# Every large tile at a multiple of 512 bytes, and new orders for the fill, the turn and the drain

## The chip, the cores and the metric

The kernel runs on one core of a Trainium2 chip. Its time is the device time of one execution in microseconds; each figure is the median of several runs. The profile is one further execution, taken by the hardware profiler.

## The reference

128 samples, each with 128 nodes of 256 features (`x`) and a weighted 128 x 128 matrix (`adj`). Four graph layers follow one another, each on the normalised and rectified features and with a residual:

```python
h = jnp.maximum(_layernorm(x, axis=-1), 0.0)
x = x + L0(h, adj, ...)   # hypergraph convolution, relu, layer norm, hypergraph convolution, + h
h = jnp.maximum(_layernorm(x, axis=-1), 0.0)
x = x + L1(h, adj, ...)   # tanh(norm(adj) @ h @ W + b)
h = jnp.maximum(_layernorm(x, axis=-1), 0.0)
x = x + L2(h, adj, ...)   # attention: exp(leaky(8 tanh((s_i + s_j) / 8))) * adj, rows rescaled, @ h @ w
h = jnp.maximum(_layernorm(x, axis=-1), 0.0)
x = x + L3(h, adj, ...)   # three layers adj @ (h @ W) + b, relu after the first two
```

All arrays are float32.

## The kernel before

Two samples (J = 2) lie side by side in a pass, and four streams A, B, C and D each take one pass after another; 16 groups of four passes make 64 passes, called units below. Each unit goes through 16 steps on TensorE (PE). A step named U multiplies by the graph's matrix in float32 (eight instructions of 128 columns; 1U has sixteen), a step named W by a weight matrix. For W each operand is split into a high and a low part of type fp32r (UHI and ULO, WHI and WLO), and the product is the sum of three: twelve matmuls of 256 columns, in 0W twelve of 512, in 1W twenty-four of 256. G makes the hypergraph's matrix, 3S spreads the attention scores, 5U works on rows with the split of T (THI, TLO). Behind every U, ScalarE (ACT) copies the result to UHI and VectorE (DVE) writes what is left to ULO; the second half of the next W waits for it. Behind every W comes a residual sum, statistics on DVE (0S, 1S, ...), a norm on GpSimd (POOL; N0 to N3, NZ) and the normalising copy on ACT (H0, 1W, 2X, 3W).

The order of each engine's work is written out by hand in the table `ORDER` (line 20): for PE, ACT, DVE, POOL and the load queue (SP) a first list, a turn that is repeated, and a last list. `ordered` (line 63) gives the n-th occurrence of a step to stream n modulo 4. The engines run in order and meet at semaphores alone, so a step that waits holds up all behind it on its engine. A turn holds one unit's steps, each of another stream or pass, so that a chain of one stream spans several turns. With the counts in the lists there are 55 turns on PE.

Names of the steps: B and G on ACT build and copy the hypergraph's matrices; `high` and `low` split a weight matrix on ACT and DVE; `shifts` (PE, once) and `centred` (DVE, once) fold the layer norm's parameters into W2 and hold one of the two wide banks until done; SH, R and TH on ACT are the residual's shift, the row sums of adj, and the high part of T; DA to DD on DVE turn degrees into factors; 2N, RX, RB, RH on POOL are weighting and residual sums. PE begins with 18 warm-up matmuls of ones.

SBUF tiles are laid out one after another in the order in which `sb(...)` is called (lines 99 to 177), each start rounded up to 32 bytes. In the kernel before, small tiles such as `COLS` (40 bytes), `L3B1C` (8) and the four constants (8 each) stand among the large ones, and `BHT` and `G` have 1040 bytes, so what follows them starts at odd places:

```python
WLO = {step: sb(f"WLO{step}", [P, *shape], F32R) for step, shape in WIDTH.items()}
COLS = sb("COLS", [P, 2 * HC + DC])
GAMMA, BETA, ACOL = COLS[:, 0:HC], COLS[:, HC:2 * HC], COLS[:, 2 * HC:]
B1 = sb("B1", [P, DH])
```

Of the kernel before, what the change touches and what calls it, by code (L numbers as in the profile page):

```python
# [6 lines left out]
F32 = mybir.dt.float32  # L7
F32R = mybir.dt.float32r
ACT = mybir.ActivationFunctionType
P = 128  # L10
J = 2
STREAMS = ("A", "B", "C", "D")
# [14 lines left out]
    "ACT": (  # L27
# [8 lines left out]
    "DVE": (  # L36
# [22 lines left out]
}  # L59


# [13 lines left out]
def program(nc, xs, adj_t, adj_r, w1t, w2t, l1w, l2w, l2wt, l3w1, l3w2, l3w3, cols, b1, b2, l1b, l3b1, l3b2, l3b3, out):  # L75
# [6 lines left out]
    with ExitStack() as ctx:  # L82
# [30 lines left out]
        def per_stream(name, *shape, dt=F32):  # L113
            return {s: sb(f"{name}_{s}", [P, *shape], dt) for s in STREAMS}
# [762 lines left out]
```

## Time and profile before

| | |
|---|---|
| median of 3 runs | 1374.74 us (1374.6 to 1374.94) |
| the profiled execution, its span | 1375.02 us, 1373.2 us |
| mean granted clock of TensorE | 0.997 |
| PE busy | 1348.1 us, 98% |
| PE's weight loads (PEld) | 1293.4 us, 94% |
| DVE, ACT, POOL busy | 1202.0 (88%), 1112.6 (81%), 1037.1 us (76%) |
| chain that ended last | PE 83%, DVE 10%, issue 3%, ACT 3%, POOL 1% |

The profiled execution's own time is 1.8 us above its span, which goes from the first to the last instruction. Matmuls overlap one another, so the distance between starts tells more than the busy time of one. The timeline merges equal instructions that follow each other; the bracket behind a row is the idle time of the engine before it and what ended it.

### The profile page before, as it was taken

What the parts mean: (1) busy time and instruction counts of PE and PEld (TensorE: products, weight loads), DVE (VectorE), ACT (ScalarE), POOL (GpSimd) and SP (SyncE); (2) the same over time, 40 slices, a digit from 0 to 9 for tenths busy, and PEclk for the clock granted to TensorE, in tenths of its full rate; (3) what the DMA queues carried; (4) which work ended last, traced back from release to release, by engine and by line L of the source; (5) the groups of instructions that cost most, each with busy time, mean ns of one, the idle gap of its engine ahead of it and who ended that gap; (6) DMA issues with size and microseconds to landing.
All of it is one profiled execution on the core that took longest, in us unless ns stands there. A gap on an engine that the chain in (4) does not pass through costs nothing.

```text
span 1373.2 us, 32422 instructions
## 1 busy us (share of the span) xinstructions
PE 1348.1 (98%) x10552; PEld 1293.4 (94%) x10552; DVE 1202.0 (88%) x3607; ACT 1112.6 (81%) x2824; POOL 1037.1 (76%) x2067
## 2 busy tenths in 40 slices
PE   8989999999999999999999999999999999999988
PEld 7879999999999999999999999999999999999987
DVE  6887988988988988988988989889889889889876
ACT  5787888888888888888887888888887888888875
POOL 5867778777777777777777777777787787777762
PEclk9999999999999999999999999999999999999999
DMA  6011111112111111111111111111111111121100
GB/s 200 13 29 54 32 36 56 47 36 55 48 36 55 48 36 56 47 36 53 49 36 48 55 36 48 43 48 47 44 48 47 37 54 48 36 55 47 36 9 32
DMA packets 83351, 64.37 MB, mean 47 GB/s; under 512 B 40560, under 2 KB 65648, under 8 KB 83184
## 3 DMA queue, kind: packets, MB, share of 16 engines
q1 hardware_dynamic: 83184, 62.29, 15.7%
q8 instruction: 86, 1.41, 0.4%
q14 instruction: 81, 0.66, 0.2%
HBM read 45.49 MB, written 16.78 MB: 45 GB/s over the span
## 4 chain that ended last, share of the span: by engine, by line
PE 83%; DVE 10%; issue 3%; ACT 3%; POOL 1%; DVEq 0%; POOLq 0%; ACTq 0%
PE BANK L394 20%; PE BANK L326 18%; PE BANK L401 12%; PE WIDE L394 8%; PE WIDE L337 8%; PE BANK L353 4%; PE WIDE L401 4%; PE BANK L358 2%; PE BANK L311 2%; PE BANK L370 1%; PE BANK L373 1%; PE BANK L369 1%; PE BANK L412 1%; DVE BN_B L594 1%; DVE ST_A L615 1%
## 5 line engine op out<-in xcount | busy, mean ns | idle before, releaser
L635 DVE TENSOR_TENSOR ULO_C<-BANK,UHI_C 128x512 fp32r<-128x512 f32 x112 | 76.5, 683 | 25.0 <-ACT UHI_C L539 15.8
L635 DVE TENSOR_TENSOR ULO_D<-BANK,UHI_D 128x512 fp32r<-128x512 f32 x112 | 76.4, 682 | 24.1 <-ACT UHI_D L539 13.0
L635 DVE TENSOR_TENSOR ULO_A<-BANK,UHI_A 128x512 fp32r<-128x512 f32 x112 | 76.5, 683 | 23.2 <-ACT UHI_A L539 11.8
L635 DVE TENSOR_TENSOR ULO_B<-BANK,UHI_B 128x512 fp32r<-128x512 f32 x112 | 76.5, 683 | 21.0 <-ACT UHI_B L539 12.3
L478 ACT ACTIVATE UHI_D<-BANK 128x512 fp32r<-128x512 f32 x96 | 57.1, 595 | 40.5 <-PE BANK L326 37.3
L478 ACT ACTIVATE UHI_A<-BANK 128x512 fp32r<-128x512 f32 x96 | 57.2, 596 | 39.6 <-PE BANK L326 38.5
L478 ACT ACTIVATE UHI_C<-BANK 128x512 fp32r<-128x512 f32 x96 | 57.1, 595 | 38.7 <-PE BANK L326 34.8
L478 ACT ACTIVATE UHI_B<-BANK 128x512 fp32r<-128x512 f32 x96 | 57.1, 595 | 35.9 <-PE BANK L326 34.5
L761 POOL TENSOR_TENSOR LN_A<-LN_A,MHALF 128x2 f32<-128x2 f32 x80 | 56.5, 706 | 1.3
L757 POOL TENSOR_TENSOR LN_B<-MV_B,EPS 128x2 f32<-128x2 f32 x80 | 15.6, 195 | 55.0 <-DVE MV_B L602 54.9
L447 ACT ACTIVATE H_A<-RES_A,LN_A 128x256 f32<-128x256 f32 x96 | 52.4, 597 | 5.4 <-POOL LN_A L769 5.0
L534 ACT ACTIVATE BANK<-BANK,L3B1C 128x256 f32<-128x256 f32 x128 | 51.9, 443 | 5.9 <-PE BANK L358 3.1
L761 POOL TENSOR_TENSOR LN_C<-LN_C,MHALF 128x2 f32<-128x2 f32 x80 | 55.5, 694 | 1.3
L761 POOL TENSOR_TENSOR LN_B<-LN_B,MHALF 128x2 f32<-128x2 f32 x80 | 55.5, 694 | 1.2
L761 POOL TENSOR_TENSOR LN_D<-LN_D,MHALF 128x2 f32<-128x2 f32 x80 | 55.5, 694 | 1.3
L447 ACT ACTIVATE H_C<-RES_C,LN_C 128x256 f32<-128x256 f32 x96 | 52.4, 598 | 1.7 <-POOL LN_C L769 1.6
L447 ACT ACTIVATE H_B<-RES_B,LN_B 128x256 f32<-128x256 f32 x96 | 52.3, 597 | 1.3 <-POOL LN_B L769 1.3
L757 POOL TENSOR_TENSOR LN_A<-MV_A,EPS 128x2 f32<-128x2 f32 x80 | 15.6, 195 | 49.9 <-DVE MV_A L602 49.9
L447 ACT ACTIVATE H_D<-RES_D,LN_D 128x256 f32<-128x256 f32 x96 | 52.3, 596 | 0.8 <-POOL LN_D L769 0.3
L757 POOL TENSOR_TENSOR LN_C<-MV_C,EPS 128x2 f32<-128x2 f32 x80 | 15.6, 195 | 48.8 <-DVE MV_C L602 48.8
L757 POOL TENSOR_TENSOR LN_D<-MV_D,EPS 128x2 f32<-128x2 f32 x80 | 15.6, 195 | 47.7 <-DVE MV_D L602 47.7
L594 DVE BATCH_NORM_STATS2 BN_A<-RES_A 128x6 f32<-128x256 f32 x96 | 35.6, 411 | 1.5 <-POOL RES_A L811 1.5
(519 smaller groups left out, 6053.6 us busy)
## 6 DMA issues: line engine op xcount, KB each, us to landing
X_A<-in_xs SPq DMA_DIRECT2D x16, 256.0 KB, 2.8
X_B<-in_xs SPq DMA_DIRECT2D x16, 256.0 KB, 2.9
X_C<-in_xs SPq DMA_DIRECT2D x16, 256.0 KB, 3.0
X_D<-in_xs SPq DMA_DIRECT2D x16, 256.0 KB, 3.0
out_rows<-O_A SPq DMA_DIRECT2D x16, 256.0 KB, 2.0
out_rows<-O_B SPq DMA_DIRECT2D x16, 256.0 KB, 2.1
out_rows<-O_C SPq DMA_DIRECT2D x16, 256.0 KB, 2.0
out_rows<-O_D SPq DMA_DIRECT2D x16, 256.0 KB, 2.0
```

What stands on the lines that cost most here:

```text
L326: last = nc.tensor.matmul(bank(s, step, k)[:, at:at + P], lhs[s][:, j, m * P:(m + 1) * P], rhs(s, j), start=True, stop=True)
L337: last = nc.tensor.matmul(bank(s, "1U", k)[:, j, m * P:(m + 1) * P], Z[s][:, j, m * P:(m + 1) * P], GZ[s][:, j, :], start=True, stop=True)
L353: nc.tensor.matmul(dst, w[:, m, q * P:(q + 1) * P], UHI[s][:, m * n:(m + 1) * n], start=(w is lo and m == 0), stop=False)
L394: nc.tensor.matmul(dst, UHI[s][:, at[m]:at[m] + P], w[:, m, :], start=(w is lo and m == 0), stop=False)
L401: last = nc.tensor.matmul(dst, ULO[s][:, at[m]:at[m] + P], hi[:, m, :], start=False, stop=(m == chunks - 1))
L447: nc.scalar.activation(dst[s][:, j, :], src[s][:, j, :], ACT.Relu, bias=LN[s][:, NB, j:j + 1], scale=LN[s][:, RSTD, j:j + 1]).then_inc(sem ...
L478: nc.scalar.activation(UHI[s][:, 0:J * D], bank(s, step, k)[:, :], ACT.Copy).then_inc(sem(f"c{step}"), 1)
L534: last = nc.scalar.activation(half, half, ACT.Relu, bias=L3B1C[:, q:q + 1])
L594: last = nc.vector.bn_stats(BN[s][:, j, :], src[s][:, j, :])
L635: nc.vector.tensor_tensor(ULO[s][:, 0:J * D], bank(s, step, k)[:, :], UHI[s][:, 0:J * D].bitcast(F32), ALU.subtract).then_inc(sem(f"l{step ...
L757: nc.gpsimd.tensor_tensor(ve, MV[s][:, :, 1], EPS[:, :], ALU.add).then_inc(sem("ve" + tag), 1)
L761: nc.gpsimd.tensor_tensor(rstd, ve, MHALF[:, :], ALU.pow)\
```

## The change

The tiles of a multiple of 512 bytes are asked for first, behind the 384 bytes of `ST`, which bring the first of them to a multiple of 512; the odd-sized ones (BHT, DIAG, G, COLS, the constants, the statistics) come last. No tile changes its size, and no instruction its operands. The first and last lists of all five engines are new. The turn lists of PE, ACT, DVE, POOL and SP stand in the diff as they were. The lists of ACT, DVE and SP are cut to the first one here, POOL's are left out.

```diff
@@ -19,43 +19,42 @@
 
 ORDER = {
     "PE": (
-         "G 0U G 0W shifts 0U G 0W 0U 1U 1W 1U G 0W 1W 0U 2U 0W 2W 1U 1W 2U 1U 2W 1W 3S 2U 3U 2W 3W 2U 3S 2W 3U 4U 3W 3S "
-         "4W G 5W 3U 4U 5U G 3W 6U 4W 6W 0U 5W 3S 0W 5U 4U 6U 4W 3U 6W 1U 0U 1W 5W 3W 0W 2U G 5U 2W 6U 1U 1W 4U 6W",
+         "G 0U G 0W 0U shifts G 0W 1U 0U 1W 0W G 1U 2U 1W 2W 0U 1U 0W 2U 1W 3S 2W 1U 3U 1W 3W 2U 3S 2W 4U 3U 4W 2U 3W G 5W "
+         "2W 3S 5U 4U 4W 6U 3U 6W 5W 3W 0U 3S 5U 0W 4U G 3U 6U 4W 6W 1U 1W 0U 5W 3W 0W 2U 5U G 2W 6U 1U 1W 4U 6W",
          "0U 4W 3S 0W 2U 5W 3U 2W 5U 3W G 6U 1U 1W 4U 6W",
-         "0U 4W 3S 0W G 3U 5W 2U 3W 5U 2W 1U 6U 4U 1W 4W 6W 0U G 5W 0W 5U 2U 3S 6U 2W 6W 1U 0U 3U 0W 1W 3W 3S 1U 2U 1W 2W "
-         "4U 3U 4W 3W 2U 2W 5W 4U 3S 4W 3U 5U 3S 3W 3U 5W 3W 5U 4U 6U 4W 4U 6U 5W 4W 6W 5U 5W 6W 5U 6U 6U 6W 6W"),
+         "G 0U 3S 4W 0W 3U 2U 5W 2W 5U 3W 1U 6U 1W G 4U 6W 0U 3S 4W 0W 5W 2U 3U 5U 2W 6U 1U 6W 0U 3W 0W 1W 3S 1U 1W 2U 3U "
+         "4U 2W 3W 2U 4W 2W 5W 4U 3S 4W 5U 3U 5W 3S 3W 3U 6U 3W 6W 4U 5U 4U 4W 4W 6U 5W 5W 5U 6W 5U 6U 6U 6W 6W"),
     "ACT": (
-         "B G high H0 B 0U G 0W H0 B 0U G high H0 0Z SH 0W 1U B 0Z SH high 0U 1U SH H0 G 0W high R 1W 0U 2U TH SH R 0Z 0W "
-         "high 1U 2W 0Z 1W high 2U 2X 1U R 2Y high 2W TH 3T 3E 1W 2U 3U 2X 1W 2W 2Y 2U 3T 3E 3W 2X 3U 2W 4U 2Y B 3T 3E 4W "
-         "4V G 3W R 5W B 3U 2X 4U 5U G H0 TH 6U 4W 4V 2Y TH 0U H0 3T 5W SH 3W 3E 5U 4U 0W 6U 4W 0Z 4V 3U 1U R SH B 0U 5W "
-         "H0 1W 0W 2U 5U 0Z 2W TH 6U",
+         "B H0 high G B 0U G H0 0U 0W B H0 G R 0Z high SH TH 1U 0U high 0W B high SH 0Z 0W 1W 1U SH high 2U high G H0 TH "
+         "0Z 2W 0U SH 1U 1W 2X 2U 0W 2Y 3T 3E 0Z 2W 1U 3U R high TH 2X 1W 2Y 2U 3T 3E 3W 2W 4U B 1W 3U 4W 4V 2X 2U R G 2Y "
+         "5W 3T 3W 3E 4U 2W 5U H0 4W 6U 4V TH 3U R 2X 5W 2Y 0U 3T 3E B 3W 5U 4U 0W G 6U 3U SH 0Z 4W 1U 4V H0 R 0U 5W B SH "
+         "1W 0W 2U H0 5U 0Z 2W TH 6U",
...
     "DVE": (
-         "T X XA DA DB DC T low spread 0U X DA scaled 0W DD DB XA X T XA 0S centred DC 0U 0A T low 0W DD 0S 0A 1U DA DB X "
-         "XA 1W DC 0U DD 1U 1S 0W 1A 0S DA 0A DB 1W DC 1S 0U DD 1A low 2U 0W 0S 2W 0A 1U low 2S 2A 1W 2U 1S 1A low 1U 2W "
-         "1W 1S 2S 2A 3L 3E 3R 1A 3I 2U 3J 3U 2W T 3W 3S 3A 2S 2A 2U 3L 3E 3R 2W 3I low 3U 3J T 4U 2S 3W 3S 3A 3L low 4V "
-         "3R 3E 2A X 3I DA 5W XA 3U 5U 3J 4U X DB DC DA 3W 6U 3S 3A DB XA 4V 6W DC 0U T DD 5W 0W 5U 3L 3E 3R 4U 0S 3I 0A "
-         "6U 4V 3U X 1U DD XA 6W 1W 0U 1S 1A 5W 3J 3W 3S 0W 0S 2U 0A 5U 2W T 3A 2S 2A 1U DA 6U 1W DB DC 1S DD 4U 6W 0U 1A "
-         "X",
+         "T X XA spread T DA low X DB XA DC 0U scaled 0W T X DA XA 0S 0A DB DD 0U T DC DD centred X DA 0W low XA 1U 0U 0S "
+         "DB 1W 0A 1S DC 1A 0W 0S low DD 0A 1U low 2U 1W 1S 2W DA 1A DB DC DD 0U 2S 2A low 1U 0W 2U 0S 0A 1W 1S 2W 3L 3R "
+         "3E 2S 1A 3I 2A 1U 3U 3J low 1W T 3W 3S 3A 2U 1S 3L 1A 2W 3E 3R 4U 2S 3I 2A 3U T 3J 4V 3W 2U 3S 3A low 5W X DA XA "
+         "2W 5U 4U 3L 3R DB 2S 3I 3E 2A 6U 4V DC 3J 3U X 6W DD 5W 3W 3S 3A 0U 5U 3L 3R T 3E 0W 4U 0S 0A 6U DA 3I 3U XA DB "
+         "6W X 1U 4V 1W 1S DC 3J 1A DD 0U 5W XA 3W 0W 0S 2U 0A 5U 2W T 3S 3A 2S 2A 1U DA 6U 1W DB 4U 6W DC DD 1S 1A 0U X",
...
     "SP": (
-         "W F F D X W F F R W X F X D D R X T T O X O R D O D W X T F T W",
+         "F X F W D R W W F F X R X D T R D X O T O X X T O F D W D T W F",
...
@@ -96,22 +95,20 @@
         WIDTH = {"0W": (DC, DH), "1W": (HC, D), "2W": (DC, D), "3W": (DC, D), "4W": (DC, D), "5W": (DC, D), "6W": (DC, D)}
         W_STEPS = tuple(WIDTH)
         U_STEPS = tuple(f"{i}U" for i in range(7))
+        def per_stream(name, *shape, dt=F32):
+            return {s: sb(f"{name}_{s}", [P, *shape], dt) for s in STREAMS}
+
+        ST = per_stream("ST", 12, J)
+        CNT, CNM, BE, DNM, DNI, DN, S2, DG1, DINV, S8, RSR, RSA = range(12)
         WHI = {step: sb(f"WHI{step}", [P, *shape], F32R) for step, shape in WIDTH.items()}
         WLO = {step: sb(f"WLO{step}", [P, *shape], F32R) for step, shape in WIDTH.items()}
-        COLS = sb("COLS", [P, 2 * HC + DC])
-        GAMMA, BETA, ACOL = COLS[:, 0:HC], COLS[:, HC:2 * HC], COLS[:, 2 * HC:]
         B1 = sb("B1", [P, DH])
         B2, L1B, L3B2, L3B3 = (sb(n, [P, D]) for n in ("B2", "L1B", "L3B2", "L3B3"))
-        L3B1C = sb("L3B1C", [P, DC])
         BW = sb("BW", [P, D])
         WA = sb("WA", [P, D])
         SPREAD = sb("SPREAD", [P, HC + DC, P])
         IDENT = sb("IDENT", [P, P])
         ONES = sb("ONES", [P, P])
-        MONE, MHALF, LEAST, EPS = (sb(n, [P, J]) for n in ("MONE", "MHALF", "LEAST", "EPS"))
-
-        def per_stream(name, *shape, dt=F32):
-            return {s: sb(f"{name}_{s}", [P, *shape], dt) for s in STREAMS}
 
         X = per_stream("X", J, D)
 
@@ -123,11 +120,8 @@
         THI = per_stream("THI", J, P, dt=F32R)
         TLO = per_stream("TLO", J, P, dt=F32R)
 
-        BHT = per_stream("BHT", J, P + 2)
-        DIAG = per_stream("DIAG", J)
         HT = per_stream("HT", J, P)
         AT = per_stream("AT", J, P)
-        G = per_stream("G", J, P + 2)
         GZ = per_stream("GZ", J, P)
         H = per_stream("H", J, D)
         H0 = per_stream("H0", J, D)
@@ -138,14 +132,21 @@
         TMP = per_stream("TMP", J, D)
         AE = per_stream("AE", J, P)
         O = per_stream("O", J, D)
+        JUNK = per_stream("JUNK", J, P)
+        W1, W2, W2G = sb("W1", [P, DC, DH]), sb("W2", [P, HC, D]), sb("W2G", [P, HC, D])
+        RAW6W = sb("RAW6W", [P, DC, D])
+        BHT = per_stream("BHT", J, P + 2)
+        DIAG = per_stream("DIAG", J)
+        G = per_stream("G", J, P + 2)
+        COLS = sb("COLS", [P, 2 * HC + DC])
+        GAMMA, BETA, ACOL = COLS[:, 0:HC], COLS[:, HC:2 * HC], COLS[:, 2 * HC:]
+        MONE, MHALF, LEAST, EPS = (sb(n, [P, J]) for n in ("MONE", "MHALF", "LEAST", "EPS"))
+        L3B1C = sb("L3B1C", [P, DC])
         BN = per_stream("BN", J, 6)
         MV = per_stream("MV", J, 2)
         LN = per_stream("LN", 4, J)
         VE, NMU, RSTD, NB = range(4)
-        ST = per_stream("ST", 12, J)
-        CNT, CNM, BE, DNM, DNI, DN, S2, DG1, DINV, S8, RSR, RSA = range(12)
         RR = per_stream("RR", J)
-        JUNK = per_stream("JUNK", J, P)
         DNS, DGH = ({s: G[s][:, :, P + i] for s in STREAMS} for i in range(2))
 
 
@@ -169,9 +170,8 @@
 
         SETUP = bank("A", "shifts", 0)
 
-        W1, W2, W2G = sb("W1", [P, DC, DH]), sb("W2", [P, HC, D]), sb("W2G", [P, HC, D])
         L2WT = TMP["D"]
-        RAW = {"0W": W1, "1W": W2, "2W": O["A"], "3W": O["B"], "4W": O["C"], "5W": O["D"], "6W": sb("RAW6W", [P, DC, D])}
+        RAW = {"0W": W1, "1W": W2, "2W": O["A"], "3W": O["B"], "4W": O["C"], "5W": O["D"], "6W": RAW6W}
 
         block = ctx.enter_context(nc.Block())
```

## Rows read from the trace of the kernel before

**Rows 1.** Windows: us, busy us of each engine (x instructions), PEclk, DMA share, GB/s.
```profile
51.00:68.00 17.00, 14.74 (x111) 14.06 (x110) 12.54 (x39) 12.65 (x34) 14.67 (x30) 0.90 0.08 25
68.00:85.00 17.00, 14.02 (x97) 12.76 (x96) 14.76 (x56) 13.84 (x41) 11.05 (x25) 0.90 0.17 47
620.74:641.48 20.74, 20.70 (x166) 19.95 (x165) 18.59 (x57) 17.23 (x45) 16.13 (x32) 1.00 0.17 47
```

**Rows 2.** Timeline of PE, the anchors: start us, us, engine line, op, out<-in, count.
```profile
8.11 0.61 PE L311 MATMUL BANK<-BHT_A,HT_A 128*128 128x130 f32 x4
...
129.22 1.06 PE L326 MATMUL BANK<-G_C,H_C 128*128 128x128 f32 x8
...
1270.08 1.05 PE L326 MATMUL BANK<-G_B,H_B 128*128 128x128 f32 x8
...
1369.48 0.40 PE L401 MATMUL BANK<-WHI6W,ULO_D 128*128 128x256 f32 x2
```

**Rows 3.** Timeline of PE, start of the fill: 0W of A, shifts, 0U of B, 1U of A.
```profile
13.55 0.71 PE L394 MATMUL WIDE<-WLO0W,UHI_A 128*128 128x512 f32 x2
...
16.44 1.89 PE L285 MATMUL WIDE<-W,SPREAD 128*128 128x256 f32 x8
...
20.75 1.05 PE L326 MATMUL BANK<-G_B,H_B 128*128 128x128 f32 x8
...
26.63 1.95 PE L337 MATMUL WIDE<-GZ_A,Z_A 128*128 128x128 f32 x16
```

**Rows 4.** Lines of ACT, shapes apart: count, busy us, mean ns, idle before.
```profile
L465 ACT ACTIVATE G_A<-BANK 128x260 f32<-128x260 f32 x16 | 6.1, 382 | 3.4 <-PE BANK L311 3.4
L465 ACT ACTIVATE G_D<-BANK 128x260 f32<-128x260 f32 x16 | 6.1, 381 | 0.0
```

**Rows 5.** Timeline of PE in one turn: 4W of C, 5U of C, 3W of D.
```profile
608.00 0.40 PE L353 MATMUL BANK<-UHI_C,WLO4W 128*128 128x256 f32 x2
...
608.48 0.40 PE L358 MATMUL BANK<-ULO_C,WHI4W 128*128 128x256 f32 x2
...
616.37 0.28 PE L369 MATMUL BANK<-UHI_C,TLO_C 128*128 128x256 f32 x1
...
617.07 0.40 PE L394 MATMUL BANK<-WLO3W,UHI_D 128*128 128x256 f32 x2
```

**Rows 6.** Timelines of POOL, ACT and DVE in the first 30 us.
```profile
6.16 0.20 POOL L769 TENSOR_TENSOR LN_A<-LN_A 128x2 f32<-128x2 f32 x1
...
9.04 1.05 ACT L441 ACTIVATE WHI0W<-W 128x1024 fp32r<-128x1024 f32 x1
...
25.98 0.69 ACT L494 ACTIVATE GZ_A<-G_A,LN_A 128x128 f32<-128x128 f32 x2 [0.86 <-POOL LN_A L761]
...
21.63 1.41 DVE L582 SCALAR_TENSOR_TENSOR W<-WIDE,W2G 128x256 f32<-128x256 f32 x4
```

**Rows 7.** Timeline of SP, then DMA issues: KB each, median us to landing.
```profile
2.97 0.47 SPq L246 DMA_DIRECT2D W<-in_w1t  x1
...
W<-in_w1t SPq DMA_DIRECT2D x1, 512.0 KB, 4.0
```

**Rows 8.** Timeline of PE, fill: 2U of C, 4U of B.
```profile
61.23 1.60 PE L326 MATMUL BANK<-AT_C,H_C 128*128 128x128 f32 x8 [2.20 <-issue]
...
84.04 1.06 PE L326 MATMUL BANK<-T_B,H_B 128*128 128x128 f32 x8
```

**Rows 9.** Timeline of PE, drain: end of the last 2W, 3S of D.
```profile
1333.18 0.40 PE L401 MATMUL BANK<-WHI2W,ULO_D 128*128 128x256 f32 x2
...
1341.74 0.43 PE L412 MATMUL BANK<-IDENT,ST_D 128*128 128x128 f32 x2 [0.79 <-ACT Z_D L505]
```

**Rows 10.** Lines of DVE: DA of stream A, count, busy us, mean ns, idle before.
```profile
L615 DVE TENSOR_SCALAR ST_A<-G_A 128x2 f32<-128x2 f32 x16 | 15.5, 970 | 4.2 <-ACT G_A L465 4.2
```

**Rows 11.** Timeline of PE in one turn: G of C and what follows.
```profile
618.48 0.61 PE L311 MATMUL BANK<-BHT_C,HT_C 128*128 128x130 f32 x4
618.93 1.09 PE L326 MATMUL BANK<-T_C,H_C 128*128 128x128 f32 x8
```

26 rows, old and new, of the table ORDER are left out of this document.

## The prediction

> **What bounds the kernel now.** I read the page's busy shares first, then windows, then TensorE's (PE) timeline. In one turn of the steady loop PE is busy 20.70 of 20.74 us at full clock [rows 1], and no other engine is over 18.6. The turn's first step starts at 129.22 us the first time and at 1270.08 the first time after the loop [rows 2]; between them lie 55 turns of 20.74 us. So PE is the bound for 1140.9 us, and an order can gain only ahead of 129.2 or behind 1270.1.
>
> How much lies there: the first real matmul starts at 8.11, the last ones at 1369.48 with an end at 1369.9 [rows 2]. Fill plus drain are (129.22 - 8.11) + (1369.9 - 1270.08) = 220.9 us. Work in them: 64 units less 55 turns leave 9 units, 9 x 20.74 = 186.7, and the one-time shifts, 16.44 to 20.75, 4.3 us [rows 3]. So 29.9 us are waits and half clock: about 20 in the fill and 10 in the drain. Two windows of the fill have a mean granted clock of 0.90, a part of each at the lower level, 1.2 GHz, after gaps of PE of over 2 us [rows 1, 8]; 0.10 x 17 us is 1.7 us lost in each, 3.4 of the 20. Ahead of 8.11 runs the warm-up, behind 1369.9 one add and the last store; the change touches neither.
>
> **The change part by part.**
>
> *Turn.* All five turn lists are the same word for word and as many steps stand in each first and last list as before, so there are again 55 turns. Cost 0.
>
> *Placement.* No instruction is added. Counting the tiles' sizes through, the big ones start 96 to 352 bytes past a multiple of 512 before and at 0 after. The trace has one comparison: the four G tiles start at four different such offsets, and the copies into them take 382, 382, 382 and 381 ns, the first and the last shown [rows 4]. No tile that matters starts at 0, so that place itself isn't seen. As bounds for PE I take the spread between its 256-column fp32r matmuls: four of 4W start 0.48 us apart in all, 120 ns each, and six of 5U take 0.70, 117 ns each [rows 5]; the two differ in operands and places. A unit has 90 of these, so if all moved by half that spread, 1.5 ns x 90 x 64 is 9 us either way. I take 0, since the only rows with nothing but the place changed show none, and keep -9 and +9. What loads gain from whole 512-byte pieces is hidden: the only early waits for a DMA, DVE's for TF_A and X_A, end before 4 us, under the warm-up.
>
> *Fill, start.* Before, ScalarE (ACT) does B, G, high, H0 for stream A: it waits for G's matmul, only then copies W1 (9.04, 1.05 us) and normalises. The new order is B, H0, high, G. LN_A is written at 6.36 and W1, issued at 2.97 with 4.0 us to landing, is there at 7.0 [rows 6, 7], so H0 runs at 6.4 and the copy at 7.5 to 8.5, both under the warm-up; G follows at 8.76 as before. 0U of A can start at 9.2, VectorE's (DVE) low part of W1 is done by 10.6, and 0W of A starts at about 11.1 instead of 13.55 [rows 3]: -2.4 us.
>
> *Shifts.* They move behind 0U of B: about 14.9 to 19.2 instead of 16.44 to 20.75. DVE's centred copies follow them and ended at 23.04, and the chain of Z_A was queued around them, so GZ_A came at 25.98 and 1U of A at 26.63 [rows 3, 6]. In the new DVE list 0S and 0A of A stand ahead of centred, so GZ_A can be done by about 21.6, when centred frees the bank too, and 1U of A starts after 0W of B at about 22.5: -4.1 us. With R and TH of stream A now early on ACT, two loads come on the path; R_A was issued at 12.5 and took 3.7 us, and ACT wants it at about 20.
>
> *Fill, 58 to 84.* Here PE lost most: 2.20 us before 2U of C [rows 8], several of 0.4 to 1.3 behind it, and the lower clock. Cause: GpSimd (POOL) had the residual sums and the weighting of H in front of the norm that 2U of C needs. In the new order 3S and 3U of A come before 1W of D, and 3W of A before 2U of C; I followed the five new queues step by step, with the durations of before, up to 4U of B. The steps on PE are priced by their distance to the next one's start in a turn: 0.81 us for the short U, 1.74 for 1U, 1.41 to 1.52 for the twelve-matmul W, 2.92 for 1W, 2.88 for 0W. PE then waits some 0.3 to 0.6 us before each of about eight steps, nowhere for 2, and 4U of B starts near 75 instead of 84.04 [rows 8], with 3U of C still to do and 5U of A done already: -9 us in all, the -4.1 included and 3.4 of it the clock, which did not fall before the long gaps.
>
> *Rest of the fill.* 4W of B now comes directly behind 4U of B and must wait for its copy (0.9 us); 3W to 4U of C has 4.5 us of work between. Before, this part lost about 4 us; I put the new at 5: +1. A walk with every queue moving at once is optimistic; I take off one more. Fill: -7, bounds -13 (two thirds of its waits) and +4 (two more gaps like that of rows 8).
>
> *Drain.* Before, the last 2W ends at 1333.41 and PE 36.5 us later [rows 9], with 31.4 us of work: 5.1 us of waits. Its 3S follows 8.3 us after it [rows 9], with 1.4 us of that waited. New: 5W A, 4U B, 3S C, 4W B, 5U A, 3U C, 5W B stand between, 7.0 us, so 1.2 us are waited here again. Then 3W C and 3U D (1.0 waited), 6U A, 3W D, 6W A, 4U C, 5U B; 4U of D needs the norm of D, 4 us after 3W of D: 0.9 waited. Both 4W, 6U B, both 5W and 5U C fill the time until 5U and 6U of D (0.8 waited). Sum of waits 3.9, but 0.5 fewer at the other steps than before: about 33.8 us instead of 36.5, -2.7; I take -2, bounds -5 and +3. Ahead of the last 2W I take no change, though 0W to 1U of D has 3.1 us of work between instead of 4.5.
>
> **Sum** against the profiled execution's 1375.02 (span 1373.2 and 1.8 around it): -7 - 2 + 0 = -9, 1366.0. The median of the three runs is 1374.74, 0.3 lower: 1365.7, said as 1366. The likeliest case's own range is 1359 to 1371, the bounds of the fill and the drain taken half way.
>
> **Rivals.**
>
> *The chains set the pace, not the order* (no change). From 2W's end to 3S, streams A to C take 12.4, 13.5 and 11.5 us in the fill before (same timeline as rows 8), and PE work between is now 9.2, 7.7 and 8.8 instead of 11.7, 8.4 and 6.9. If these lengths are DVE's and POOL's load there and not their order, the waits become 3.2 + 5.8 + 2.7 = 11.7 instead of 10.4, the gain at the start is waited off by 70 us, and only the drain is left: 1373. For it: POOL is busy 14.67 of 17 us from 51 to 68 [rows 1]. Against: in the drain the same chain takes 8.3.
>
> *The turn gets longer* (slower). PE's only wait in a turn is at 6W for DVE's low part, about 0.3 us. DVE's DA, two elements, takes 970 ns on average where it takes 0.15 alone [rows 10], because a GpSimd instruction runs beside it, and it stands just ahead of 6U's low part. If the new places of ST and G shift who goes first, PE waits longer in each of 55 turns. From 9 / 55 = 0.16 us a turn it eats the gain; at 0.3 us it is 16.5, 1366 + 16.5 = 1382.5. For it: the queue there has no slack. Against: the same-offset test above, and DVE has 2.1 us free in a turn.
> The Trainium skill, "SBUF — State Buffer", section "Who interferes with whom", says that a VectorE tensor_scalar may take the port pair that it shares with GpSimd, and that the second to issue blocks until the first is done; the trace agrees with its 970 ns. By that rule the order of issue counts and the place in SBUF doesn't, which is why this rival gets a small chance.
>
> *The place speeds up the matmuls* (much faster). A 256-column fp32r matmul takes 118 ns on average of rows 5, while the four instructions of G, 130 columns each, take 0.45 us, 112 ns each [rows 11]. If misplaced reads cost the 6 ns, a unit gains 90 x 6 and 12 x 12 ns for the 512-column ones, 0.68 us, x 64 = 44 us: 1322. For it: no row explains the 6 ns otherwise. Against: tiles of W and of UHI lie at different offsets and their spacings hardly differ.
> The Trainium skill, "TensorE: Matmul & The Clock Gate", section "Back-to-back issue gap", gives 262 cycles for 256 columns, as an estimate 109 ns at 2.4 GHz; the trace shows 117 to 120. By that rule some 8 ns of each are lost to something, and this rival would have its room.
>
> *The fill gets worse* (slower): the early R, TH or F on an in-order queue holds what is behind it, 2 to 6 us in one place, while half of the gain stays off: 1378.
>
> **How the numbers follow.** Forecast (1359 to 1371) 0.57; no change or nearly (1372 to 1377) 0.17; longer turn 0.08; worse fill 0.10; faster matmuls 0.08, of which half only by a part. What a measurement can tell here is about 0.2%, 2.7 us. Faster: 0.57 + 0.08 + 0.04 of the second case = 0.69. Same: 0.13. Slower: 0.08 + 0.10 = 0.18. The range goes from 1355, which takes in 9 us of the place on top of the likeliest, to 1377; outside are the slower cases in most of their width and the large gain, about 2 in 10.
>
> **What would show it.** The turn's first step at about 122 instead of 129.2 (fill), 1140.9 us of turns after it (place), and 98 instead of 99.8 from there to the last matmul (drain). 0W of A at 11.1 and 1U of A at 22.5; no wait of PE over 1.3 us between 30 and 90, and a granted clock of 1.00 there. It is wrong if the turns differ from 20.74 by more than 0.05 us, or if 2U of C or 3S of B again waits for over 2 us.

## The result, and the profile after

The changed kernel takes 1365.57 us (median of 4 runs, 1365.48 to 1365.67), the kernel before 1374.84 beside it: a ratio of 0.9931, 95% interval 0.9914 to 0.9948. The forecast was 1366.0. Run again beside a later set the same kernel took 1368.17 (1366.56 to 1368.22), ratio 0.9941 (0.9929 to 0.9954); where that difference comes from is followed below.

From the page after: busy time, share and count of each engine, then the shares of the chain that ended last.

```profile
PE 1347.6 (99%) x10552; PEld 1296.0 (95%) x10552; DVE 1200.2 (88%) x3607; ACT 1113.7 (82%) x2824; POOL 1037.4 (76%) x2067
...
PE 92%; DVE 3%; POOL 1%; ACT 1%; issue 1%; DMA 0%; SPq 0%; DVEq 0%; POOLq 0%; ACTq 0%
```

The busy times are nearly those of before; the chain is PE for 92% instead of 83%. What went are waits. The windows of after, as in [rows 1]:

```profile
51.00:68.00 17.00, 15.95 (x124) 14.56 (x123) 15.22 (x55) 14.99 (x40) 14.30 (x32) 1.00 0.17 40
68.00:85.00 17.00, 14.85 (x115) 13.70 (x114) 14.53 (x47) 14.06 (x41) 11.07 (x21) 1.00 0.17 41
...
620.74:641.48 20.74, 20.74 (x167) 20.03 (x166) 18.60 (x56) 17.22 (x45) 16.12 (x33) 1.00 0.16 46
```

The clock stays at its upper level in both windows of the fill (0.90 before). The third shows PE busy 20.74 of 20.74 us, before 20.70: there is no room, and yet, as the next rows tell, a turn has grown. PE's timeline after; the rows answer to [rows 2, 3, 8, 9]:

```profile
8.00 0.61 PE L311 MATMUL BANK<-BHT_A,HT_A 128*128 128x130 f32 x4
...
11.02 0.70 PE L394 MATMUL WIDE<-WLO0W,UHI_A 128*128 128x512 f32 x2
...
14.17 1.05 PE L326 MATMUL BANK<-G_B,H_B 128*128 128x128 f32 x8
15.06 1.89 PE L285 MATMUL WIDE<-W,SPREAD 128*128 128x256 f32 x8
...
22.59 1.61 PE L337 MATMUL WIDE<-GZ_A,Z_A 128*128 128x128 f32 x13
...
59.65 0.35 PE L326 MATMUL BANK<-AT_C,H_C 128*128 128x128 f32 x1
...
74.87 1.21 PE L326 MATMUL BANK<-T_B,H_B 128*128 128x128 f32 x8 [0.41 <-ACT H_B L447]
...
120.76 0.28 PE L326 MATMUL BANK<-G_C,H_C 128*128 128x128 f32 x1
...
1262.93 0.28 PE L311 MATMUL BANK<-BHT_C,HT_C 128*128 128x130 f32 x1
...
1322.80 0.40 PE L401 MATMUL BANK<-WHI2W,ULO_D 128*128 128x256 f32 x2
1324.37 0.50 PE L394 MATMUL BANK<-WLO5W,UHI_A 128*128 128x256 f32 x2 [1.17 <-ACT UHI_A L539]
...
1360.16 0.40 PE L401 MATMUL BANK<-WHI6W,ULO_D 128*128 128x256 f32 x2
```

The turn starts at 120.76 instead of 129.22 (-8.5 us). Between 120.76 and 1262.93 lie 1142.2 us instead of 1140.9 (+1.3). From there to the end of the last matmul, 1360.56, it is 97.6 instead of 99.8 (-2.2). The sum, -9.4, is the difference of the spans (1363.9 and 1373.2) to 0.1. PE's longest waits after, first from 24 to 123 us, then in the drain (whom it waited for: us in total, times, longest):

```profile
PE BANK L326 <- DVE AE_C L686: 0.9, 1, 0.9
PE BANK L353 <- ACT UHI_B L478: 0.7, 1, 0.7
...
PE BANK L326 <- DVE AE_D L686: 1.3, 1, 1.3
PE BANK L394 <- ACT UHI_A L539: 1.2, 1, 1.2
PE WIDE L337 <- ACT GZ_D L494: 1.1, 1, 1.1
```

### The profile page after: what moved, and what is told of

Same layout as the page of the kernel before. It is cut to its first block, busy times and chain, and to the rows that moved or that the text cites. A ratio compares the mean times of both kernels' runs of the same rounds, so it can differ in the third digit from the quotient of the medians.

```text
span 1363.9 us, 32419 instructions
## 1 busy us (share of the span) xinstructions
PE 1347.6 (99%) x10552; PEld 1296.0 (95%) x10552; DVE 1200.2 (88%) x3607; ACT 1113.7 (82%) x2824; POOL 1037.4 (76%) x2067
## 3 DMA queue, kind: packets, MB, share of 16 engines
q8 instruction: 86, 1.41, 0.4%
## 4 chain that ended last, share of the span: by engine, by line
PE 92%; DVE 3%; POOL 1%; ACT 1%; issue 1%; DMA 0%; SPq 0%; DVEq 0%; POOLq 0%; ACTq 0%
PE BANK L394 26%; PE BANK L326 20%; PE BANK L401 14%; PE WIDE L394 8%; PE WIDE L337 8%; PE BANK L353 4%; PE WIDE L401 4%; PE BANK L358 2%; PE BANK L311 2%; PE BANK L373 1%; PE BANK L369 1%; PE BANK L370 1%; PE BANK L412 1%; DMA COLS<-in_cols 0%; DVE BN_C L594 0%
## 5 line engine op out<-in xcount | busy, mean ns | idle before, releaser
L594 DVE BATCH_NORM_STATS2 BN_D<-RES_D 128x6 f32<-128x256 f32 x96 | 35.4, 410 | 1.5 <-POOL RES_D L811 1.5
```

The source lines that it names most:

```text
L594: last = nc.vector.bn_stats(BN[s][:, j, :], src[s][:, j, :])
```

## The experiments

The last three columns are read from the profiled execution of each kernel: the start of the turn's first step, the time of the 55 turns, and from there to the end of the last matmul. The sets e, f (with after_again) and g ran on three chips, the kernel before beside each: 1375.42 us with e, 1375.55 with f, 1375.80 with g. Each ratio is to the one beside it. Two profiled executions of the changed kernel differ by 0.3 us in the turns (1142.2 and 1142.5), so much less than that is not told apart by one profile.

| kernel | median us (from, to) | ratio to before, 95% | first turn at | 55 turns | drain |
|---|---|---|---|---|---|
| before | 1374.84 | 1 | 129.22 | 1140.9 | 99.8 |
| after | 1365.57 (1365.48, 1365.67) | 0.9931 (0.9914, 0.9948) | 120.76 | 1142.2 | 97.6 |
| e1_place | 1377.33 (1377.07, 1378.41) | 1.0013 (1.0004, 1.0022) | 130.09 | 1142.4 | 100.8 |
| e2_lists | 1365.60 (1364.58, 1366.91) | 0.9928 (0.9914, 0.9941) | 121.61 | 1141.2 | 97.6 |
| e3_fill | 1367.36 (1366.77, 1368.48) | 0.9940 (0.9928, 0.9953) | 120.74 | 1141.6 | 99.8 |
| e4_drain | 1373.21 (1372.66, 1373.52) | 0.9982 (0.9973, 0.9990) | 129.33 | 1141.0 | 97.6 |
| after_again | 1368.17 (1366.56, 1368.22) | 0.9941 (0.9929, 0.9954) | 122.98 | 1142.5 | 97.6 |
| f1_act | 1366.66 (1366.51, 1367.87) | 0.9937 (0.9925, 0.9950) | 122.75 | 1142.4 | 97.6 |
| f2_norm | 1370.77 (1369.42, 1374.49) | 0.9970 (0.9961, 0.9979) | 125.52 | 1142.4 | 97.6 |
| f3_shifts | 1371.45 (1370.64, 1374.84) | 0.9973 (0.9963, 0.9983) | 126.55 | 1142.4 | 97.6 |
| g1_tb_old | 1364.29 (1364.18, 1364.33) | 0.9916 (0.9903, 0.9930) | 120.44 | 1141.2 | 97.5 |
| g2_tb_new | 1365.45 (1365.17, 1365.66) | 0.9925 (0.9913, 0.9937) | 120.73 | 1142.1 | 97.6 |
| g3_tb_128 | 1365.40 (1365.29, 1365.57) | 0.9925 (0.9911, 0.9938) | 120.61 | 1142.1 | 97.6 |
| g4_tb_u224 | 1361.17 (1361.00, 1361.19) | 0.9894 (0.9880, 0.9907) | 120.41 | 1138.4 | 97.3 |

### The parts of the change alone

e1_place has the new order of the `sb(...)` calls and the old `ORDER`, e2_lists the reverse. e3_fill and e4_drain have the old places; on all five engines e3_fill has the first list of after and the last of before, e4_drain the first of before and the last of after. The load queue's lists as an example (the other four engines' are left out):

```diff
 "SP"    e3_fill, first list
-"W F F D X W F F R W X F X D D R X T T O X O R D O D W X T F T W"
+"F X F W D R W W F F X R X D T R D X O T O X X T O F D W D T W F"
 "SP"    e4_drain, last list
-"R O O O O O D D D W W W T T T T F F X X R R R R"
+"O R O O O O D D D W W W T T T T F F X X R R R R"
```

> The new places alone, all lists as before. Theory (the places set TensorE's spacing, and nothing else of them shows): a turn of 20.767 us as in the changed kernel, 55 x 0.024 = +1.3 us, and the fill and the drain as before (turn's first step at 129.2, 99.8 us from the drain's start to the last matmul): 1376.1. Rival 1 (the longer turn is left over from the new first list, which hands the turn another phase): 20.743 us a turn, 1374.8. Rival 2 (the places also take part of the fill's waits away, through the loads or through who goes first at the port that VectorE and GpSimd share): turn's first step before 128, time under 1374.

> The new lists alone, all tiles where they were before. Theory: the turn is back at 20.743 us and fill and drain are as in the changed kernel (turn's first step at 120.8, 97.6 us from the drain's start): 1.3 us less than the changed kernel, 1364.3, faster than both. Rival 1 (the longer turn comes from the new first list): a turn of 20.767 us and 1365.6. Rival 2 (the lists need the places, since they were walked with other durations): fill over 123 us to the turn's first step, time over 1367.

> The five new first lists alone; last lists and places as before. Theory (fill and drain are separate, 55 turns between them forget everything): -8.5 us, 1366.3, with the turn's first step at 120.8 and 99.8 us from the drain's start to the last matmul. Rival (the drain's waits depend on the phase in which the fill left the other engines): 97.6 to 102 us for the drain, so 1364 or 1368.5.

> The five new last lists alone; first lists and places as before. Theory: -2.2 us, 1372.6, turn's first step at 129.2 and 97.6 us from the drain's start to the last matmul. Rival (what the drain gained came with the places or the new first lists): 99.8 us, 1374.8.

The turn's first step and the drain's first step in e1_place, then in e2_lists, then in e4_drain:

```profile
130.09 0.28 PE L327 MATMUL BANK<-G_C,H_C 128*128 128x128 f32 x1
...
1272.49 0.27 PE L327 MATMUL BANK<-G_B,H_B 128*128 128x128 f32 x1
```

```profile
121.61 0.27 PE L325 MATMUL BANK<-G_C,H_C 128*128 128x128 f32 x1
...
1262.85 0.27 PE L310 MATMUL BANK<-BHT_C,HT_C 128*128 128x130 f32 x1
```

```profile
129.33 0.27 PE L313 MATMUL BANK<-G_C,H_C 128*128 128x128 f32 x1
...
1270.31 0.27 PE L298 MATMUL BANK<-BHT_C,HT_C 128*128 128x130 f32 x1
```

The drain's gain is whole in e4_drain (97.6) and nil in e3_fill (99.8): the two ends don't know of each other. The fill's gain is whole in e3_fill without the places. The turns: 1142.4 with the new places and old lists, 1141.2 with the old places and new lists, so most of the 1.3 us is the places. The new first list may leave 0.4 to 0.8 us behind in the turns (e2_lists, e3_fill); that stays open. e1_place is slower than before by more than the turns, 1.9 us in the medians, in the trace 0.9 more in the fill and 1.0 in the drain. I had not expected that part, and its profiled execution is the longest of the eleven. The windows show a lower clock in both places: 0.57 from 12 to 16 us and 0.91 from 1332 to 1352, where before has 1.00. That the places cause this part is not shown. e2_lists came near its 1364.3 in its two shortest executions only (1364.6). Its median is that of the changed kernel, because its executions scatter over 2.3 us; that was the question for the next two sets.

### Steps of the fill undone one at a time

The lists are cut to the steps that move:

```diff
 "ACT"   f1_act
-"B H0 high G B 0U G H0
+"B G high H0 B 0U G H0
 "POOL"  f2_norm
-"RH N2 N1 2N DI TB N3
+"RH N2 2N DI N1 TB N3
 "PE", "DVE"  f3_shifts
-"G 0U G 0W 0U shifts G
+"G 0U G 0W shifts 0U G
-XA 0S 0A DB DD 0U T DC DD centred X DA
+XA centred DB DD 0U T DC DD 0S 0A X DA
```

> The changed kernel itself, unaltered, beside the three that follow and on their chip, and on the chip of before. Expected: 1365.6 to 1366, turn's first step within 1 us of 120.8, a turn of 20.767. If its own fill scatters by more than 1 us between executions (the kernel with the new lists in the old places scattered from 1364.6 to 1366.9), differences between places or single steps below 1 us are not told apart by one profile.

> The changed kernel, with ScalarE's first four steps as before the change: B G high H0 instead of B H0 high G. Theory of the prediction (what is gained at the start stays gained to the loop): 0W of A starts at 13.4 instead of 11.0, and what follows on TensorE with it, so the turn's first step at 123.2 and 1368.0. Rival 1 (the chains set the pace: later steps wait for VectorE and GpSimd anyway, so the 2.4 us are waited off): 120.8 to 121.3, 1365.7 to 1366.2. Rival 2 (the shifts, which wait for nothing, take up the slack in part): half of it, 122 and 1366.8.

> The changed kernel, with one step of GpSimd's first list moved: the norm that 2U of C needs comes behind the weighting of H of B (1.28 us) and the degree step of D (0.69). Theory (GpSimd's order was what cost 2.2 us before 2U of C): TensorE waits 1.5 to 2 us before 2U of C, which starts at 61.3 instead of 59.7, and the turn's first step comes 1.5 us later, 122.3; time 1367.1. Rival 1 (TensorE has other reserves behind it, the wait is taken back by the waits that follow, 0.9 to 1.4 us each before 85 us): turn's first step at 120.8 to 121.2, time as the changed kernel. Rival 2 (a wait of that length also drops the clock to its lower level for a while): 1.7 us more, 124.

> The changed kernel, with the one-time shifts ahead of 0U of B on TensorE again, and on VectorE the centred copies ahead of the statistics of Z of A, as before. Theory (the prediction's second term, 1.7 of its 4.1 us): Z of A's statistics end 1.9 us later, 1U of A starts at 24.3 instead of 22.6, and the turn's first step comes 1.7 us later, 122.5: 1367.3. Rival 1 (1U of A is late by something else, such as ScalarE's R step waiting for its load): 1U of A at 22.6 and no change. Rival 2 (late here, but waited off by 120): 1U of A at 24.3 and 120.8.

**after_again** shows where the scatter begins. First the changed kernel as profiled at first, then again; GpSimd's power step on ST_B (L784) and VectorE's low part of W1 (L559) in the order in which they start, then PE's G of B:

```profile
8.93 0.70 POOL L784 TENSOR_TENSOR ST_B<-ST_B,MONE 128x2 f32<-128x2 f32 x1
9.29 1.22 DVE L559 TENSOR_TENSOR WLO0W<-W,WHI0W 128x1024 fp32r<-128x1024 f32 x1
...
10.50 0.69 PE L311 MATMUL BANK<-BHT_B,HT_B 128*128 128x130 f32 x4 [0.26 <-ACT BHT_B L460]
```

```profile
8.87 1.22 DVE L559 TENSOR_TENSOR WLO0W<-W,WHI0W 128x1024 fp32r<-128x1024 f32 x1
9.10 1.56 POOL L784 TENSOR_TENSOR ST_B<-ST_B,MONE 128x2 f32<-128x2 f32 x1
...
11.52 1.21 PE L311 MATMUL BANK<-BHT_B,HT_B 128*128 128x130 f32 x4 [1.70 <-ACT BHT_B L460]
```

And a window of after_again, the 4 us behind that row:

```profile
12.00:16.00 4.00, 4.00 (x15) 3.30 (x14) 2.38 (x6) 1.37 (x3) 0.92 (x4) 0.65 1.06 263
```

Where VectorE starts first, the two-element power step takes 1.56 us instead of 0.70 and ends behind it, B of the second stream is late, and G of B waits 1.70 us. In this execution PE's clock was then granted 0.65 in the next 4 us (part of it at 1.2 GHz). In e2_lists' execution the power step took 1.70 us too, PE waited the same 1.70 us, and the clock stayed at 1.00; its waits before that were shorter (0.48 us against 1.19). What came first goes with the end of the warm-up, which PE's first G follows: 6.87 here and 8.00 there. With it G of A was copied earlier, VectorE was free earlier, and the low part came ahead of the power step. The other profiles of this order of T and spread agree: the power step took 0.70 us where the first G starts at 7.98 or later (after, e3_fill, f2_norm), and 1.56 to 1.78 where it starts at 7.79 or earlier (e2_lists, f3_shifts, after_again, f1_act); on two of the chips both occurred. An earlier PE made a later kernel. The executions of the new lists lie in three bands that fit this: with the old places 1364.6, 1365.6 (profiled: late, clock 1.00) and 1366.9; with the new ones 1365.5 (profiled: not late), 1366.6 and 1368.2 (profiled: late, and the lower clock).

**f1_act** settles nothing: its profiled execution has the late power step as well, and 0W of A starts at 12.24 there, 12.38 in after_again. Its median is 1.5 us below that of the changed kernel beside it, where 2.4 us more were forecast, so in these executions the step shows no price. The 2.4 us of the prediction for it could not be isolated.

**f2_norm**: the timeline with GpSimd's weighting of H of B, its norm of C and PE's 2U of C, then a window:

```profile
58.46 1.30 POOL L818 TENSOR_TENSOR Z_B<-H_B,WA 128x512 f32<-128x512 f32 x1 [1.57 <-ACT H_B L447]
59.71 0.69 POOL L788 TENSOR_TENSOR ST_D<-ST_D,MHALF 128x2 f32<-128x2 f32 x1
60.37 0.20 POOL L757 TENSOR_TENSOR LN_C<-MV_C,EPS 128x2 f32<-128x2 f32 x1
...
62.64 1.62 PE L326 MATMUL BANK<-AT_C,H_C 128*128 128x128 f32 x6 [3.04 <-issue]
```

```profile
51.00:68.00 17.00, 13.26 (x90) 12.48 (x89) 11.32 (x41) 11.15 (x31) 11.35 (x25) 0.81 0.17 40
```

PE waits 3.04 us instead of the 1.5 to 2 expected: the weighting put in front waits itself, 1.57 us for H of B, and hands its wait on. The turn starts 4.8 us later: 3.0 for the gap and 1.8 because the steps behind it run at the lower clock (0.59 on the mean from 62.6 to 69.7 us), the 1.7 of the second rival. (The window's mean of 0.81 would be 0.19 x 17 = 3.2 us. Part of that took the place of waits that PE has there in the changed kernel: from 2U of C to 3U of B it is 5.3 us there and 7.1 here.) Nothing is taken back. That the waits behind would swallow it (the rival) is wrong; that GpSimd's order made the old gap before 2U of C holds. The executions of f2_norm spread over 5 us and those of f3_shifts over 4; the profiled ones lie near the medians, and the longest have none.

**f3_shifts**: the timeline with GpSimd's power step on ST_B, PE's 0W of A, VectorE's centred copy, PE's G of C, VectorE's statistics of Z of A and PE's 1U of A, then a window, then 1U of A in e2_lists:

```profile
9.09 1.78 POOL L784 TENSOR_TENSOR ST_B<-ST_B,MONE 128x2 f32<-128x2 f32 x1
...
12.23 0.69 PE L394 MATMUL WIDE<-WLO0W,UHI_A 128*128 128x512 f32 x2
...
20.24 1.41 DVE L582 SCALAR_TENSOR_TENSOR W<-WIDE,W2G 128x256 f32<-128x256 f32 x4
...
22.77 0.72 PE L311 MATMUL BANK<-BHT_C,HT_C 128*128 128x130 f32 x4 [2.35 <-issue]
...
22.96 1.28 DVE L594 BATCH_NORM_STATS2 BN_A<-Z_A 128x6 f32<-128x512 f32 x2
...
27.64 1.95 PE L337 MATMUL WIDE<-GZ_A,Z_A 128*128 128x128 f32 x16
```

```profile
24.00:28.00 4.00, 4.00 (x15) 3.13 (x15) 2.17 (x9) 2.84 (x9) 3.17 (x8) 0.66 0.19 64
```

```profile
23.54 1.95 PE L336 MATMUL WIDE<-GZ_A,Z_A 128*128 128x128 f32 x16
```

1U of A starts 5.0 us later than after's 22.59, the turn 5.8. Not all of that is the price of the step: this execution has the late power step as well (1.78 us), and its 0W of A starts 1.2 us behind after's. In e2_lists, late too and at clock 1.00, 0W of A starts at 12.21; beside it 1U of A is 4.1 us later and the turn 4.9. I had expected 1.7, for Z's statistics alone. Those start at 22.96, but 0U of B was late too; ScalarE has B of C behind its copy, so G of C waited 2.35 us. Behind that wait the granted clock was 0.66, and 0W of B took 4.4 us to the next step instead of 2.9. The direction is shown; the size is that of the queues behind both steps and of the clock behind their wait.

### The race taken away, and where the tiles lie

All four have the second T of VectorE's first list a step earlier. g1 has the old places, g2 the new ones, g3 the new ones with ST last, g4 the new ones with odd-sized tiles around U:

```diff
-"T X XA spread T DA low X
+"T X XA T spread DA low X
 # g3: large tiles at 128 past a multiple of 512
-        ST = per_stream("ST", 12, J)
         WHI = {step: ...}
...
         RR = per_stream("RR", J)
+        ST = per_stream("ST", 12, J)
 # g4: U alone at 224
+        MV, L3B1C, COLS      # 224 bytes, moved here
         UHI = per_stream("UHI", J * DH, dt=F32R)
         ULO = per_stream("ULO", J * DH, dt=F32R)
+        BN, 32 bytes of pad  # 288 bytes
```

> The new lists with the tiles in their old places, and one step of VectorE's first list moved: the second T (members of B) stands ahead of spread, not behind it. Theory of the scatter (GpSimd's power step on ST_B, 0.70 us alone, starts within 0.2 us of VectorE's 1.22 us low part of W1; where VectorE is first, it takes 1.6 to 1.8 us and G of B waits 1.7 us, and in some executions the clock falls after that): with the step 1 us earlier the two no longer meet, the power step takes 0.70, G of B follows 0U of A with no wait over 0.3 us, 0W of A starts by 10.8, and all executions lie within 0.5 us, at 1364.2 (the lowest of the new lists in old places was 1364.6). Rival 1 (VectorE's six spread instructions hold the same port): the power step waits there instead, up to 1.3 us, and the scatter stays. Rival 2 (the scatter comes from when the warm-up ends and the clock alone): executions still from 1364.6 to 1366.9.

> The changed kernel with the same step moved (second T ahead of spread). Theory: no scatter either, and slower than the kernel with the old places by the turns alone, 55 x 0.02 = 1.1 us: 1365.3. Rival (the places have no cost of their own, the differences so far were the scatter): equal within 0.3 us.

> As the one before, but the 384 bytes of ST lie behind the large tiles, so that all of these start 128 bytes past a multiple of 512 and keep their distances from each other. Theory 1 (what counts is where the streamed operand itself starts): the W steps go back to the spacings of the old places (3W 1.413 us from its first matmul to the next step, 0W 2.885), a turn of 20.74 to 20.76. Theory 2 (what counts is the distance between the streamed and the stationary operand, which is 0 here as in the changed kernel): 3W 1.441, 5U 0.720, 0W 2.856, a turn of 20.77.

> As the changed kernel with T ahead of spread, but the eight U tiles alone start 224 bytes past a multiple of 512, as before the change; W and all others at 0. Theory 1 (place of the streamed operand): 4W and 5U, which stream U, go back to 1.52 and 0.700 us, the steps that stream W stay at 1.441 (3W) and 2.856 (0W). Theory 2 (distance between the two, or place of the stationary one): the W steps, whose stationary operand is U, change too, 3W towards 1.413 and 0W towards 2.885.

g1_tb_old, the power step and G of B, then g2_tb_new, PE's G of A and the power step:

```profile
8.14 0.87 POOL L783 TENSOR_TENSOR ST_B<-ST_B,MONE 128x2 f32<-128x2 f32 x1
...
9.89 0.69 PE L310 MATMUL BANK<-BHT_B,HT_B 128*128 128x130 f32 x4
```

```profile
6.73 0.61 PE L311 MATMUL BANK<-BHT_A,HT_A 128*128 128x130 f32 x4
...
8.39 0.87 POOL L784 TENSOR_TENSOR ST_B<-ST_B,MONE 128x2 f32<-128x2 f32 x1
```

In g1 the power step ends before the low part starts, G of B follows with no wait shown, 0W of A starts at 10.71, and the executions of each of the four kernels lie within 0.5 us. (0.87 instead of 0.70: the first rival, the spread instructions, costs 0.17.) In g2 the first G starts at 6.73, earlier than in after_again, and the power step is not late even so. That speaks for the race as the cause of the scatter. One thing stays open: the four ran on a chip on which the changed kernel itself was not run. Without the race, new against old places is 1365.45 against 1364.29, in the traces 0.95 us in the turns: the places cost about 1 us.

Which place counts? 3W of D from its first row to the next step's, in after, in g3_tb_128 and in g4_tb_u224; then g4's turn and drain starts:

```profile
609.14 0.40 PE L394 MATMUL BANK<-WLO3W,UHI_D 128*128 128x256 f32 x2
...
610.58 0.50 PE L311 MATMUL BANK<-BHT_C,HT_C 128*128 128x130 f32 x3
```

```profile
608.96 0.40 PE L394 MATMUL BANK<-WLO3W,UHI_D 128*128 128x256 f32 x2
...
610.40 0.50 PE L311 MATMUL BANK<-BHT_C,HT_C 128*128 128x130 f32 x3
```

```profile
607.23 0.39 PE L395 MATMUL BANK<-WLO3W,UHI_D 128*128 128x256 f32 x2
...
608.63 0.50 PE L312 MATMUL BANK<-BHT_C,HT_C 128*128 128x130 f32 x3
...
120.41 0.27 PE L327 MATMUL BANK<-G_C,H_C 128*128 128x128 f32 x1
...
1258.80 0.27 PE L312 MATMUL BANK<-BHT_C,HT_C 128*128 128x130 f32 x1
```

1.44 us in after and in g3, 1.40 in g4; before it was 1.41 (617.07 to 618.48, [rows 5, 11]). Moving everything by 128 bytes (g3 beside g2) changes no step's median by more than 2 ns. Moving U, with four kinds of small tiles set around it, changes every step that reads U. Medians over the turns, from a step's first matmul to the next step's, with the distance in bytes (modulo 512) between U and the weights, and for 5U between U and T:

| | before | after, g3 | g4 |
|---|---|---|---|
| U from W; U from T | 96; 384 | 0; 0 | 224; 224 |
| 3W, 2W, 5W | 1.413, 1.513, 1.495 | 1.441, 1.514, 1.518 | 1.398, 1.485, 1.488 |
| 4W | 1.520 | 1.512 | 1.502 |
| 1W | 2.92 (g1: 2.96) | 2.97 | 2.91 |
| 5U | 0.700 | 0.720 | 0.711 |
| 0W (512 columns) | 2.885 | 2.856 | 2.885 |

Theory 1 of g3 and g4 (where the streamed operand starts) falls: by it 3W would have gone back to 1.413 us in g3 and stayed at 1.441 in g4. Of the second, the place of the stationary operand alone does not do it either: U starts at the same place modulo 512 in before and in g4, and 3W differs by 15 ns, 2W by 28; and 5U, whose stationary operand is T, changed in g4, where T stayed. The distance fits all three layouts. Of 1W's growth, 0.04 us came with the new lists alone (g1 has the old places). g4's turn is 20.698 us instead of g2's 20.766, 55 x 0.068 = 3.7 us, and the kernel, 1361.17, beats both in the same set: 14.6 us under before (1375.80), 4.3 under g2, with no overlap of executions. Beside the old places with the same lists (g1) it is 3.1 us.

## Why the prediction was right, and where it was not

**The total.** That 1365.6 lies within 0.4 us of 1366.0 is luck in part: the fill gave 1.5 us more than forecast, and the turns took 1.3 back. In the profiled execution with the late power step the same kernel is at 1368.2. The fill's mechanism was right; the placement's argument and the drain's place were not.

**Turn lists, 0; placement, 0.** Wrong by +1.3 us: 1142.2 instead of 1140.9. The bound taken for it, half the spread between 120 and 117 ns, held the answer, but the step failed at its argument: equal copies of four G tiles at four offsets [rows 4] speak of ScalarE, not of PE. 3W and 5U, 117 to 118 ns a matmul before, now run at 120.0. The net is small because 0W gained 29 ns, and 6U and 6W (with its wait) became some 30 ns shorter each. The limit set ("wrong if the turns differ from 20.74 by more than 0.05") was not reached: 20.767.

**Fill, start, -2.4.** 0W of A at 11.02 (forecast 11.1) in the first profile. In the second it was 12.38. The sum was right for an order of two queues that it did not know to be a matter of chance. That ScalarE's four steps are what gained it is not shown, since f1_act could not isolate them.

**Shifts, -4.1 with the start.** 1U of A at 22.59 (forecast 22.5), shifts at 15.06 (14.9). f3_shifts shows that the step is on the path, and that undone it costs more than its term, 1.7: 4.1 us at 1U of A beside an execution with the same late power step, some 1.5 of them by the lower clock.

**58 to 84 us, -9 in all.** 4U of B at 74.87 (forecast 75), no wait over 0.9 us, clock 1.00. f2_norm shows the cause named, GpSimd's order. The clock's part, 3.4 us from two windows' means, is not shown by itself: a gap whose window shows 3.2 cost 1.8 in f2_norm, because slower steps also take the place of waits. And the gaps of over 2 us that the prediction names lie in the first of the two windows only; the longest in the second is 1.28.

**Rest of the fill, +1 and +1 for optimism.** From 4U of B to the turn it is 45.9 instead of 45.2 us: +0.7. The first was right; the second was not needed. Fill -8.5 instead of -7.

**Drain, -2.** The sum is right (-2.2, alone in e4_drain too), its place is not, so the number was met by luck. From the last rows of the last 2W to the end it was 36.7 us (1333.18 to 1369.88) and is 37.8 (1322.80 to 1360.56), with the same steps in it; the prediction had 2.7 less there. From the drain's start to these rows, where it took no change, it is 59.9 us instead of 63.1. (The prediction's 1333.41 for the end of 2W is the start of 5W, the step behind it.) 5W of A waited 1.2 us for its copy behind the last 2W, and 4W of B and 5U of A 0.5 each, where none was seen; 3U of D waited 1.3 us for AE_D (1.0 forecast).

**Rivals.** "The chains set the pace" fell: waits not made at 20 us are not made up by 70. "The turn gets longer" came, but by matmul spacing and 0.024 us, not by VectorE's DA and 0.3. "The place speeds up the matmuls" fell for this change, which slowed them, and yet there was 3.7 us in it for another layout (2.8 in the turns beside the old places). "The fill gets worse" fell.

## What to carry to other kernels

Where one in-order engine bounds the loop, hand-written orders are worth what its waits ahead of and behind the loop are worth. A walk of the queues with measured durations found the fill's here to 1.5 us; it met the drain's sum, but with the waits in the wrong places. Look in the walk for two engines that may meet within a few tenths of a microsecond: their order is chance here, and a meeting that held an instruction of 0.70 us back by 0.9 to 1.1 us cost up to 2.5. A layout rule by alignment alone is not one: large tiles at multiples of 512 bytes cost about 1 us here. Measure the spacing of the bound engine's instructions for a few distances between its operands.

## What the runs showed of the hardware

- The distance between U's place and that of the other operands counts: with 0 the 256-column fp32r matmuls of 3W start exactly 120 ns apart, with 96 or 224 bytes about 117. For 512 columns it is the other way about, 2.856 against 2.885 us for twelve. A shift of all large tiles together by 128 bytes changed nothing (g3); other shifts, and so places within 128 bytes, were not tried. That it is the two operands of one matmul, and not U against a third tile that another engine uses, was not tried, nor were other distances. The Trainium skill, "SBUF — State Buffer", section "Who interferes with whom", gives TensorE two read ports, for the streamed operand and for the weight load, and calls them independent. By that rule the distance would change nothing; g4 against g3 differs by 43 ns in twelve matmuls, and the measurement decides.
- A two-element GpSimd instruction takes 0.70 us, or 1.56 to 1.78 when VectorE's subtraction of two SBUF operands (1.22 us) started between 0.23 us before it and 0.01 us behind it (four profiles). The Trainium skill, "SBUF — State Buffer", section "Who interferes with whom", says that a VectorE instruction with two SBUF inputs contends with a GpSimd one that reads SBUF; the traces agree, with these numbers.
- The same kernel was 2.5 us slower (1368.17 against 1365.67 in the profiled executions) where its warm-up ended 1.1 us earlier (6.87 against 8.00). By the start of the turn 2.2 of them are there: 1.0 at G of B, by that order, and 1.2 in G of B and 0W of A, by the lower clock. Why the warm-up's end moves was not tested. The Trainium skill, "TensorE: Matmul & The Clock Gate", Part 1 on the clock gate, says that the number of matmuls at the lower clock at a kernel's start differs from run to run; the two ends of one warm-up of 18 agree with that.
- With a gap of PE of 3.04 us the mean clock of its 17 us window was 0.81, and the work behind took 1.8 us more; gaps up to 0.9 us in the changed kernel's fill left it at 1.00. From 12 to 16 us it was 0.65 behind gaps of 1.19 and 1.70 us (after_again) and 0.69 behind 2.00 and 0.93 (f1_act), but 1.00 behind 0.48 and 1.70 (e2_lists) and 0.63 and 1.69 (f3_shifts).
